# The last six layer-2 product chunks of the last block: made by GpSimd instead of VectorE

## The reference

```python
x0 = prev = inputs                       # (B, 39, 16)
for i, f in enumerate([128, 128, 128]):
    h = prev.shape[1]                    # 39, then 64, 64
    Wr = Ws[i].reshape(h, 39, f)
    z = relu(einsum('bhk,bmk,hmf->bfk', prev, x0, Wr) + bs[i][None, :, None])
    results.append(z[:, :64])
    prev = z[:, 64:]
return sum(concatenate(results, axis=1), axis=-1) @ W_lin
```

## Time and profile before

| | us |
|---|---|
| median of 3 runs | 2015.1 |
| lowest and highest | 2013.05, 2015.74 |
| the profiled execution's own time | 2011.91 |
| its span in the trace | 2010.1 |
| PE busy | 1998.9 (99%) |
| DVE busy | 1791.3 (89%) |
| ACT busy | 520.2 (26%) |
| POOL busy | 2.2 |

### The profile page before, as it was taken

One profiled execution on the slowest core, in us unless ns is written; L12 is line 12 of the kernel. 1 busy time (PEld: TensorE's weight loads), 2 busy tenths in 40 slices (PEclk: granted clock), 3 DMA queues, 4 the chain that ended last, 5 costly groups with the idle time before them and its releaser, 6 DMA issues.

```text
span 2010.1 us, 19878 instructions
## 1 busy us (share of the span) xinstructions
PE 1998.9 (99%) x6328; PEld 803.8 (40%) x6328; DVE 1791.3 (89%) x1184; ACT 520.2 (26%) x485; POOL 2.2 (0%) x7
## 2 busy tenths in 40 slices
PE   8999999999999999999999999999999999999999
PEld 3344333444333443334433344433444333443343
DVE  7988998888988889888898888898888988889888
ACT  2331133321233212333113332133321233311332
POOL 0000000000000000000000000000000000000000
PEclk9999999999999999999999999999999999999999
DMA  7967976668766678666786667876678866678610
GB/s 186 214 139 155 195 151 143 149 145 187 168 145 144 148 170 186 140 149 144 156 194 146 147 143 152 187 166 147 140 151 171 180 150 141 148 156 194 148 36 1
DMA packets 98877, 307.11 MB, mean 153 GB/s; under 512 B 19281, under 2 KB 20178, under 8 KB 98860
## 3 DMA queue, kind: packets, MB, share of 16 engines
q1 hardware_dynamic: 98012, 306.69, 70.3%
q10 hardware_dynamic: 848, 0.20, 0.1%
HBM read 306.81 MB, written 0.01 MB: 153 GB/s over the span
## 4 chain that ended last, share of the span: by engine, by line
PE 97%; DVE 2%; DMA 1%; issue 0%; ACTq 0%; SPq 0%; ACT 0%; DVEq 0%
PE acc L465 68%; PE acc L535 25%; PE acc L459 3%; DVE prod L296 1%; PE acc L544 1%; DMA x_seed<-x 0%; DVE x_bc L258 0%; DVE prod L302 0%; DMA prod<-x 0%; PE acc L477 0%; DVE x_rot L268 0%; SPq L203 0%; PE acc_y L589 0%; ACTq L646 0%; PE acc L595 0%
## 5 line engine op out<-in xcount | busy, mean ns | idle before, releaser
L296 DVE TENSOR_TENSOR prod<-prev,x_bc 128x2048 f32<-128x2048 f32 x512 | 1138.1, 2282 | 4.2 <-PE acc L465 4.2
L465 PE MATMUL acc<-prod,w_sb 128*128 128x512 f32 x2432 | 1052.5, 594 | 0.2 <-DVE prod L296 0.2
L465 PEld LDWEIGHTS acc<-prod,w_sb 128*128 128x128 f32 x2432 | 460.0, 190 | 592.3 <-issue 562.9
L535 PE MATMUL acc<-prod,w_sb 128*64 128x512 f32 x2432 | 530.0, 594 | 1.3 <-DVE prod L296 1.3
L605 ACT ACTIVATE prev<-acc,bias 64x1024 f32<-64x1024 f32 x128 | 142.0, 1109 | 1310.5 <-PE acc L465 1290.2
L465 PE MATMUL acc<-x_rot,w_sb 117*128 117x512 f32 (+1 forms) x768 | 335.9, 593 | 3.3 <-DVE x_rot L268 3.3
L535 PEld LDWEIGHTS acc<-prod,w_sb 128*64 128x64 f32 x2432 | 171.4, 137 | 356.0 <-issue 302.1
L610 ACT ACTIVATE prev<-acc,bias 32x1024 f32<-32x1024 f32 x256 | 283.2, 1106 | 4.0
L302 DVE TENSOR_TENSOR prod<-prev,x_bc 128x1024 f32<-128x1024 f32 x192 | 228.7, 1217 | 1.5
L465 PEld LDWEIGHTS acc<-x_rot,w_sb 117*128 117x128 f32 (+1 forms) x768 | 145.5, 190 | 188.9 <-issue 188.1
L268 DVE TENSOR_TENSOR x_rot<-x_rot,x_rep 124x1024 f32<-124x1024 f32 (+1 forms) x188 | 216.0, 1217 | 0.0
(11 more groups left out here) (39 smaller groups left out, 100.6 us busy)
## 6 DMA issues: line engine op xcount, KB each, us to landing
x_bc<-x SPq DMA_DIRECT2D x310, 256.0 KB, 10.8
x_bc<-x SPq DMA_DIRECT2D x155, 512.0 KB, 18.7
x_rot<-x SPq DMA_DIRECT2D x186, 312.0 KB
x_rot<-x SPq DMA_DIRECT2D x192, 156.0 KB
x_bc<-x SPq DMA_DIRECT2D x124, 128.0 KB, 6.7
x_rep<-x SPq DMA_DIRECT2D x62, 192.0 KB
x_rep_s<-x SPq DMA_DIRECT2D x64, 128.0 KB, 22.3
x_rot_s<-x SPq DMA_DIRECT2D x64, 128.0 KB, 22.4
```

Of the source, the lines that this page charges most:

```text
L296: mul = nc.vector.tensor_tensor(prod[:, s:s + w, :], twice, x_bc[:, u, t:t + w, :], ALU.mult)
L465: mm = nc.tensor.matmul(acc[:, h, :], w, rhs[:, BANK * h:BANK * h + BANK], start=start, stop=stop)
L535: mm = nc.tensor.matmul(acc2[HALF * h:HALF * h + HALF, u, :], w2_sb[:, ORDER[pos], :], prod[:, pos % RING, BANK * h:BANK * h + BANK], star ...
```

## The change

In the last block, DVE makes only the first nine runs of layer 2 (positions 0 to 13). GpSimd makes positions 14 to 19, one instruction of 128x1024 for each, into the six slots of `x_rot`, after it has waited for the block's `x_bc` loads, for the last layer 0 to be done and for both halves of `prev[1]`. TensorE takes positions 14 to 19 of the last block from `x_rot`, and waits for a new semaphore, `pool_ready`, for each.

```diff
+    POOL_RUNS, POOL = 9, 14
...
+        pool_ready = sem("pool_ready")
...
-            products2(LAST, 1, n + 3 * CH)
+            products2(LAST, 1, n + 3 * CH, range(POOL_RUNS))
...
             nc.gpsimd.memset(x_seed[:], 0.0).then_inc(seed_cleared, 1)
+
+            for g in range(len(XB_GROUPS)):
+                pool.wait_ge(bc_loaded[1][g], STEPS * (16 * BC_LOADS[g]))
+            pool.wait_ge(acc0_full, LAST + 1)
+            pool.wait_ge(prev_ready[1], LAST * 2 + 2)
+            for pos in range(POOL, CH):
+                a, t = CHUNKS[ORDER[pos]]
+                nc.gpsimd.tensor_tensor(x_rot[:, pos - POOL, :], prev[1][a][:], x_bc[:, 1, t, :],
+                                        ALU.mult).then_inc(pool_ready, 1)
...
                 for pos in part:
-                    pe.wait_ge(prod_ready, runs + RUN_OF[pos] + 1)
+                    if opened and pos >= POOL:
+                        pe.wait_ge(pool_ready, pos - POOL + 1)
+                        made = x_rot[:, pos - POOL, :]
+                    else:
+                        pe.wait_ge(prod_ready, runs + RUN_OF[pos] + 1)
+                        made = prod[:, pos % RING, :]
                     for h in range(NH):
                         mm = nc.tensor.matmul(acc2[HALF * h:HALF * h + HALF, u, :], w2_sb[:, ORDER[pos], :],
-                                              prod[:, pos % RING, BANK * h:BANK * h + BANK],
+                                              made[:, BANK * h:BANK * h + BANK],
```

## The result

The changed kernel takes 2025.35 us (median of 6 runs, 2023.14 to 2027.35) where the kernel before takes 2015.09: ratio 1.0054, 95% interval 1.0044 to 1.0064, so 10.3 us slower. The profiled execution took 2023.14 us, its span is 2021.3.

A forecast was written before the change was run, and what follows sets the result against it. PE's matmuls bound nearly everywhere, DVE's products the last 21 us. Five POOL instructions (+12.0 us) less the 1.46 us gain gave +10.5 us on 2015.1: 2025.6 us, range 2012.8 to 2029.0.

The forecast's parts named there:

- The limit of the gain: Last block, PE's last eight chunks in one piece from position 12: at most 1.46 us gained.
- Exclusion: Last block's layer 2: DVE and POOL products exclude each other and alternate, five POOL instructions before 12-13, 12.0 us.
- the first L376: Program start: DVE instruction of 1292 ns against 464 ns, read as held up 0.83 us by POOL's memset.
- The price d: Time of one 128x1024 POOL product in the last block: 0.95 to 2.86 us, with 5d = 12.0 us.
- third rival: PE's last eight chunks: TensorE's clock falls after idling, +3.5 to +6.9 us on top of the forecast; chance 0.10.
- PE's order: Last block: PE takes positions in order, six POOL chunks behind position 12; eight chunks from 2008.5 take 7.09 us.
- The tail: PE's L535, L589 and L595 behind the last block's chunks: keeps its length.
- VectorE's sums: DVE's channel sums behind the last products, 3.5 us: end before 2014.4, ahead of PE's L589, so hidden.
- First rival: Last block: no exclusion between DVE and POOL products, so -1.46 us, 2013.6 us; chance 0.22.
- Second rival: Last block: DVE keeps its turn, POOL starts only at 1996.5: +7.0 us, 2022.1; chance 0.16 together with sharing.

The follow-up runs named there:

- fourth experiment: Changed kernel with the last block's layer-2 rows written to PSUM for VectorE: 28.0 us from `left2` to the span's end; ratios 0.9990 and 0.9991 to the kernel before.
- e6_order: Changed kernel with TensorE taking the last block's GpSimd positions between the others as they are made: median 2018.58 us, ratio 1.0021 to the kernel before.

## Why the prediction was right

The mechanism, its place and its sign were the forecast's, and the median came out at 2025.35 for 2025.6 us. That closeness is in part two errors that cancel.

- **The limit of the gain** was 1.46 us; with memsets, and with VectorE reading PSUM, 1.4 us were measured in the last stretch.
- **Exclusion** held: five products grew by one GpSimd instruction each, in strict turns, and VectorE's 4-5 went first, as said. POOL's starts lay 4.36 us apart, where 3.5 to 4.6 was the sign named for it. But the row it rested on is not the row that proves it. The prediction read the earlier trace rows as a memset, which only writes, holding up a VectorE instruction with one input; the experiments show that memsets do not hold up VectorE's products at all, while a copy does. Whatever made the first L376 long (the two rows look the same in every kernel here, and no run moved the memset, so the cause stays open), it is not what holds up the products. Drawn from this row, the conclusion was luck; the prediction had said that the row doesn't prove it. The condition is what the experiments show: VectorE's products, with both inputs in SBUF, against a GpSimd instruction that reads SBUF. The five runs that varied either side agree (0 us for a memset, 0.84 for a copy, 2.17 for a product of other data, 0 with one input in PSUM, twice).
- **The price d** stands in the forecast's sum as 2.4 us (5d = 12.0), between the ends 0.95 and 2.86. It was the author's estimate, and no run shows that figure. Measured, it is 2.17 us as VectorE feels it and 2.30 from one to the next alone. Mis-sized term: 5 x (2.4 - 2.17) = 1.15 us too much.
- **The clock** stood as the third rival, with a chance of 0.10 and a price of 3.5 to 6.9 us. It did fall, which was that rival's own sign, and cost 1.6 us in the last eight chunks (8.69 us, where the forecast's sign was one piece of 7.1; 1.7 given back by the idle matmuls). The rival was much too improbable and its price too high: the clock came back during the eight chunks. With both mended: 5 x 2.17 - 1.46 + 1.6 = 11.0 us, which is the 11.0 of the trace. The half speed of that price is granted nowhere in the rows of before: the program's first four matmuls took 0.9 us each, but the granted clock of the first 5 us is 1.00 in the trace. The changed kernel shows the level: at 0.50 eight matmuls took 3.54 us, where eight took 1.94 at 1.00.
- **PE's order** carried its part: eight chunks behind position 12. Of the loss, 5.5 us go away when PE takes chunks as they come.
- The tail kept its length, and VectorE's sums stayed hidden (L355 ended at 2011.86, PE wanted them at 2016.14), although L366 was held up 1.0 us.
- **First rival**: it needed the two engines to run side by side. That they can, with one VectorE operand in PSUM, and then take 28.0 us, is what the fourth experiment showed. **Second rival**: GpSimd did get its turns at once (starts at 1985.55 and 1989.98), so its +7.0 did not come; forced by a wait it came as +7.5.
- Two slips change nothing: 3 x 0.95 is 2.85, not 2.86, and the chances of the slower cases add up to 0.76, not 0.75.

## What to carry over

GpSimd is no spare VectorE for two-input work: while both read SBUF, a 128x1024 product on GpSimd takes 2.17 us from VectorE, in which VectorE makes two such products itself (a start every 2.20 us). Look at what each instruction reads before splitting work: the same split ran fully side by side once VectorE's second operand lay in PSUM (8.88 us for four VectorE products, 14.0 for six of GpSimd's). And where a slower producer's chunks are put at the end of TensorE's order, everything behind the late chunk is lost with it: order the consumer by when things are ready.

## What was not expected of the hardware

TensorE's clock fell earlier than the gap that the prediction feared: in the changed kernel it was at the half level (0.50) by 1997.5, after idle times of 1.19 and 2.43 us with 1.9 us of matmuls between, while at the start of the program a gap of 3.03 us was followed by matmuls at a granted clock of 1.00 (twelve in 5.39 us). With two GpSimd chunks it fell to 0.50 behind the same two gaps (1.19 and 2.42 us), with copies (0.50 too) behind gaps of 1.10, 0.90 and 1.96 us, and with GpSimd's products alone behind each other, single chunks (1.08 us) between gaps of 1.23 us, by the fifth of them (0.50 from 2011 on). With gaps of at most 1.13 us (e6_order) it never fell. But the gaps alone do not say when. With products of other data PE had the same 1.19 us, 1.94 us of matmuls and 2.43 us, and the clock was still full (1.00) 4 us later. It fell in the gap of 2.21 us that followed one of 1.36 (stretches as above):

```profile
2003.00:2004.00 1.00, 0.77 (x4) 0.00 (x0) 1.00 (x1) 0.00 (x0) 1.00 (x1) 1.00 0.00 0
2004.00:2005.00 1.00, 0.00 (x0) 0.00 (x0) 1.00 (x1) 0.00 (x0) 1.00 (x2) 0.61 0.00 0
```

The last eight chunks took 9.12 us there, against 8.69 in the changed kernel, though VectorE and GpSimd worked alike. No run here shows what sets the moment.

A GpSimd copy holds a VectorE product up by only 0.84 us, less than a memset of the same tile takes (0.95 in the earlier trace rows, 5.42 / 6 = 0.90 in the last stretch); how long a copy takes by itself no run shows. And the duration that the profile gives a GpSimd instruction contains its wait: 4056 ns on average for what takes 2.30 us alone.
